# One eviction order for ScalarE in every slot of a hand-scheduled Flamingo-style block

## What is computed

```python
x = x + tanh(g0) * cross_attention_16_heads(layernorm(x), ctx)     # q, k, v projections, softmax, out projection
x = x + tanh(g1) * real(ifft(fft(layernorm(x)) @ w)) + bias        # becomes one 256x256 matrix, "fmix"
x = x + tanh(g2) * one_head_attention(layernorm(x), ctx, ctx)
t = rmsnorm(x); route = top 4 of 16 experts by t @ gate_w
x = x + tanh(g3) * sum over the 4 experts of route_e * mlp2_e(swiglu(mlp1_e(t)))
```

## Time and profile before

| | |
|---|---|
| median of 3 runs | 1135.19 us (1132.16 to 1136.17) |
| the profiled execution's own time | 1136.17 us |
| its span, first to last instruction | 1134.4 us, so 1.8 us lie around it |
| granted TensorE clock over the span | 0.98 |
| busy: TensorE, VectorE, ScalarE, GpSimd | 92%, 72%, 63%, 46% |

### The profile page before, as it was taken

One profiled execution on the slowest core, in us unless ns is written; L12 is line 12 of the kernel. 1 busy time (PEld: TensorE's weight loads), 2 busy tenths in 40 slices (PEclk: granted clock), 3 DMA queues, 4 the chain that ended last, 5 costly groups with the idle time before them and its releaser, 6 DMA issues. The chain is left out here.

```text
span 1134.4 us, 22413 instructions
## 1 busy us (share of the span) xinstructions
PE 1039.8 (92%) x7055; PEld 957.5 (84%) x7055; DVE 813.1 (72%) x2017; ACT 716.6 (63%) x1853; POOL 521.5 (46%) x747
## 2 busy tenths in 40 slices
PE   4899999999999999999999999999998778859995
PEld 4899898989889988889898988898897767858993
DVE  4656786868777787878686878677876865846665
ACT  4645766676766767676767676676766545635661
POOL 5413245445454635454545445463534225544441
PEclk9999999999999999999999999999998889989999
DMA  6332122222323232222222222212213522344469
GB/s 175 99 110 59 43 57 65 56 63 59 78 56 81 53 79 65 69 61 61 64 54 70 60 53 58 64 50 62 54 46 93 180 62 89 116 111 156 135 191 315
DMA packets 77569, 98.47 MB, mean 87 GB/s; under 512 B 14459, under 2 KB 69373, under 8 KB 77200
## 3 DMA queue, kind: packets, MB, share of 16 engines
q1 hardware_dynamic: 68064, 79.04, 26.3%
q0 software_dynamic: 8848, 16.96, 4.3%
q10 hardware_dynamic: 544, 1.05, 0.3%
HBM read 44.08 MB, written 23.03 MB: 59 GB/s over the span
## 5 line engine op out<-in xcount | busy, mean ns | idle before, releaser
L935 POOL TENSOR_TENSOR prob<-prob,rinv 112x750 f32<-112x750 f32 x128 | 184.1, 1438 | 250.3 <-DVE rinv L1609 239.8
L1027 ACT ACTIVATE prob<-ps_s,negmax 112x375 f32<-112x375 f32 x256 | 143.9, 570 | 61.5 <-DVE negmax L1603 52.4
L1616 DVE TENSOR_TENSOR pT_lo<-ps_pt,pT_hi 125x672 fp32r<-125x672 f32 x128 | 108.5, 847 | 63.1 <-ACT pT_hi L1164 57.7
L1707 PE MATMUL ps_kv<-ctxT_hi,wkv 128*128 128x376 f32 x512 | 138.5, 351 | 2.1 <-DVE v_lo L1276 1.4
L1603 DVE TENSOR_REDUCE negmax<-ps_s 112x2 f32<-112x750 f32 x128 | 119.0, 930 | 1.6 <-PE ps_s L1955 1.5
L1707 PE MATMUL ps_kv<-wkv,ctxT_hi 128*125 128x512 f32 x384 | 110.7, 410 | 2.4 <-DVE k_low L1272 2.4
L1017 ACT ACTIVATE v_hi<-ps_kv 125x512 fp32r<-125x512 f32 x96 | 57.3, 597 | 80.9 <-PE ps_kv L1707 75.8
L894 POOL DMA_INDIRECT places<-ysb,place_i x72 | 70.9, 984 | 81.1 <-issue 43.0
L1965 PE MATMUL ps_pt<-ident,prob 112*125 112x112 f32 x768 | 104.4, 272 | 2.3 <-POOL prob L935 2.3
L1164 ACT ACTIVATE pT_hi<-ps_pt 125x672 fp32r<-125x672 f32 x128 | 93.6, 731 | 5.7 <-PE ps_pt L1965 1.1
L1965 PEld LDWEIGHTS ps_pt<-ident,prob 112*125 112x125 f32 x768 | 94.8, 190 | 2.6 <-POOL prob L935 2.5
(11 more groups left out here) (312 smaller groups left out, 2752.8 us busy)
## 6 DMA issues: line engine op xcount, KB each, us to landing
kx<-k_low SPq DMA_DIRECT2D x256, 94.0 KB
xg<-rows_by_expert SPq DMA_DIRECT2D x72, 128.0 KB
qx_hi<-qx_hi SPq DMA_DIRECT2D x64, 112.0 KB, 2.2
zb<-places SPq DMA_DIRECT2D x16, 448.0 KB, 15.7
ctx_in<-in_ctx SPq DMA_DIRECT2D x16, 375.0 KB
stage_w<-in_L_ffn_mlp_w SPq DMA_DIRECT2D x16, 256.0 KB, 5.3
arena<-in_L_ffn_mlp_w SPq DMA_DIRECT2D x16, 256.0 KB, 5.8
stage_w<-in_L_xattn_w_kv SPq DMA_DIRECT2D x4, 512.0 KB, 11.9
```

What stands on the lines that cost most here:

```text
L935: e_prob.done(eng.tensor_tensor(prob[0:TQ, p % 2, :, :], prob[0:TQ, p % 2, :, :], rinv[:, 2 * p:2 * p + 2].unsqueeze(2).broadcast_to([TQ, ...
L1027: e_exp.done(eng.activation(prob[0:TQ, p % 2, half, :], S[0:TQ, half, 0:SK], ACT.Exp, bias=negmax[:, h:h + 1], accum_out=rowsum[:, h:h + 1]))
L1616: e_pt_lo.done(eng.tensor_tensor(pT_lo[:, :, :, :].rearrange("p h k t -> p h (k t)"), PT[0:KEYT, :, 0:NKEY * TQ], pT_hi[:, :, :, :].bitcas ...
L1707: last = eng.matmul(out_, lhs(i, k), rhs(j, k), start=(n == 1), stop=(n == KT * len(PASSES)))
```

## The change

ScalarE's program had two orders, by the parity of the slot. In even slots it did `oT`, `tail`, the expert tile, the projection evictions, then the exponents, then `pT_hi`. In odd slots it did `oT`, `tail`, exponents, `pT_hi`, the tile, the projection evictions. The change keeps the second order for all slots, and folds neighbouring loops over the pairs into one, on ScalarE, VectorE and TensorE:

```diff
@@ ScalarE @@
-                if g % 2 == 0:
-                    (oT of pair p)
-                    tail(g)
-                    for k in SLOT_TILES.get(g - LAST_BODY, ())[:1]:
-                        tile(k)
-                    for step, kind, n in kv_groups(g):
-                        projection(step, kind, n)
-                    (exponents of pair p)
-                    (pT_hi of pair p)
-                    tail_end(g)
-                else:
-                    (oT), tail(g), (exponents), (pT_hi), tile(k), projection(...), tail_end(g)
+                (oT of pair p)
+                tail(g)
+                for p in range(NP):
+                    st = due(g, AT_S[p])
+                    if st:
+                        exponents(st, p)
+                    st = due(g, AT_PT[p])
+                    if st:
+                        (pT_hi of pair p)
+                for k in SLOT_TILES.get(g - LAST_BODY, ())[:1]:
+                    tile(k)
+                for step, kind, n in kv_groups(g):
+                    projection(step, kind, n)
+                tail_end(g)
@@ VectorE @@
                         e_max.done(eng.tensor_reduce(negmax[:, 2 * p:2 * p + 2], S[0:TQ, :, 0:SK], AX.X,
                                                      ALU.max, negate=True))
-                for p in range(NP):
                     st = due(g, AT_S[p] + 1)
```

More of the change, by code:

```diff
@@ new lines, in _ @@
+                for p in range(NP):
+                    st = due(g, AT_O[p] + 1)
+                    if st:
+                        e_o.wait_ge(eng, st, p + 1)
+                        for half in range(2):
+                            rows_ = slice(64 * half, 64 * half + 64)
+                            last = eng.activation(oT[rows_, p, :], OT[rows_, half * TQ:(half + 1) * TQ],
+                                                  ACT.Copy)
+                        e_oT.done(last)
+                tail(g)
@@ new lines, in _ @@
+                for p in range(NP):
+                    st = due(g, AT_S[p])
+                    if st:
+                        exponents(st, p)
+                    st = due(g, AT_PT[p])
+                    if st:
+                        e_pt_pe.wait_ge(eng, st, p + 1)
+                        e_o.wait_ge(eng, st, p)
+                        e_pt_hi.done(eng.activation(
+                            pT_hi[:, :, :, :].rearrange("p h k t -> p h (k t)"),
+                            PT[0:KEYT, :, 0:NKEY * TQ], ACT.Copy))
```

## The result

The changed kernel takes 1161.08 us (median of 4, 1159.02 to 1163.83) against 1135.09 us (4 runs, 1132.16 to 1136.17): ratio 1.0239, 95% interval 1.0215 to 1.0262. It is slower, by 26 us where 7 were predicted. Its profiled execution took 1160.28 us with a span of 1158.5, so the two spans differ by 24.1 us.

What follows compares the result with a forecast made beforehand. TensorE was taken to bound the kernel; 15 rows x 0.4 = 6.0 us, first row 1.1 and slot 12 0 gave +7.1, or 1142 us against the median; forecast's own range 1139 to 1145, with rivals 1130 to 1149.

Steps and rivals of the forecast that it cites:

- Folded loops cost nothing, the exchange on ScalarE is all: All engines: folded loops keep their instruction order at no cost; only exponents going ahead of projection evictions in even slots remains.
- Slots 2 and 4, n1 late by 0.4 us: VectorE's delay from v2's late eviction reaches `x1` and n1: about 0.4 us a row, 6.0 us over 15 rows.
- the wait for `pT_lo` in slot 8: Sign of being right: a new TensorE wait in slot 8, where `pT_lo` had a margin of 0.05 us.
- First row +1.1 us: First batch row: GpSimd's L946 follows v2's late low part, so TensorE's wait for probabilities grows by 1.1 us.
- Slot 10: "nothing, with almost no margin": v5's eviction moves from 596.60 to about 597.9; its low part ends at about 599.2, bank wanted at 599.3.
- The `nT` wait stays, as slot 13's 0.57 us of idle time takes up the delay: ScalarE leaves slot 12 0.5 us late; idle time before q0's eviction absorbs it, leaving TensorE's slot 14 wait unchanged.
- a rival for gains: ScalarE's waits go away: `xnT` and `nT` waits of 11.1 and 6.7 us shrink, 1117 to 1130 us; chance 0.19.
- Slot 12: 0 to 0.1 us a row: c1's late eviction: low part ends at about 605.3, k0's product wants it at 605.33; summed as 0, bound 1.5 us.
- slots 10 and 12 hurt as well: Rival: c1's low part or v5's bank is late and the `nT` wait grows, another 7.5 us, 1150; chance 0.14.
- The rule that the prediction weighed for L1290: Slot 5's VectorE L1290 is held by GpSimd's L819 through shared SBUF ports: term stays 6 us, otherwise 1.5 us.

Runs made afterwards that it cites:

- x6: Kernel before, with the fourth choice's two scatters issued in slot 15, not 12, in all rows but the last; 1127.33 us, ratio 0.994.
- x1: Kernel before, with the new order (exponents ahead of evictions) in slot 10 alone; 1153.93 us, ratio 1.0152.
- x9: x7 with the new order in slot 10 alone; 1127.13 us, ratio to before 0.9941.
- x12: x7 with the new order in slots 6, 12 and 14 alone; 1136.2 us, ratio to before 1.0027.
- x8: Changed kernel with the scatters at x7's places; 1141.08 us, ratio to before 1.0089.
- x4: Changed kernel, with the row scatters of choices 2 and 3 issued in slots 14 and 15, entry scatters left in place; 1155.96 us, ratio 1.0168.
- x7: Kernel before, with second, third and fourth choice's scatters at offsets 43, 47, 48, not 42, 43, 44, except in the last row; 1121.01 us, ratio 0.9912.
- x13: x1 with the last choice's row scatter moved two slots later, to slot 14, its entry scatter left in slot 12; 1133.18 us, one run.
- x14: x13 plus a plain GpSimd write of the same 112 rows in the row scatter's old place; 1132.2 us, one run.

## Why the prediction was wrong, point by point

- *Folded loops cost nothing, the exchange on ScalarE is all*: right. The instruction sequences of all other engines are those of before.
- *Slots 2 and 4, n1 late by 0.4 us*: right. `x1` 0.36 late, TensorE +0.35 from slot 6 to 8 (0.4 predicted). TensorE gives all of it at n1, so the wait for `pT_lo` in slot 8, one of the prediction's signs, does not come.
- *First row +1.1 us*: too small. It went from 57.48 to 59.47 us. This row's interval 12 to 14 falls at about 8.5, 10.1 or 11.7 us (before 10.14, after 8.40, x6 11.74), whatever the order; without that interval the growth is 3.7 us.
- *Slot 10: "nothing, with almost no margin"*: **this is the step that failed.** Most of its numbers were right: v5's eviction 1.2 us late, `oT` unmoved. The bank of v5 had a little less than the margin that it needed. The context transposes that take it next start 6.15 us after the scores in place of 6.06, only 0.15 us behind the end of v5's low part. I put the +0.11 from 10 to 12 down to that, and in row 12 of after the profile names this wait (0.27 us for `v_lo`). But that is the small part. What I did not follow is VectorE behind v5's low part: its reciprocal for slot 11 is 1.22 us late, GpSimd's probabilities with it, and the two pairs of scatters that GpSimd issues behind them. I had asked of every moved instruction who wants its result, and not what is queued behind it on VectorE and then on GpSimd. The term stood at nothing and measured 0.94 us a row in the changed kernel. x1 gives the price alone, 17 us, and x9 shows that in a steady row it is paid only through those scatters.
- *The `nT` wait stays, as slot 13's 0.57 us of idle time takes up the delay*: wrong. That idle time, called a wait for q0's product, was the hold itself and grew to 1.32 us. The record of the `xnT` side had the same sign, and the prediction noted it ("what held it is not fully shown"), but built a rival for gains on it, not one for losses.
- *Slot 12: 0 to 0.1 us a row*: right for the bank (x12: 7.83 from 12 to 14 against 7.66, 0.17) and wrong beyond it: 0.45 us a row through `k_low` (x12), hidden in the changed kernel by the `nT` wait.
- *The rival "slots 10 and 12 hurt as well", 1150 at 0.14*, named the right place and the right wait. Its price of 0.5 us a row was half of the 0.94 measured, and its way, c1's low part or v5's bank, wasn't the one: v5's bank gave the 0.11.

The measured parts of a steady row, 0.35 + 0.11 + 0.94 = 1.40 us, would be 21 us over 15 rows. The body grew by 20.0. The first row gave more (1.99 us), rows 1, 2, 12 and 13 less (0.52, 0.73, 0.45 and 0.89); 2 and 12 of before (53.94 and 54.10 us) were held already. After the last score, after takes 258.6 us and before 254.0 (4.6 us; the first score comes 0.5 us sooner in after). There the granted clock was 0.90 in after and 0.95 in before. The windows from 900 us to the end, before and then after (stretch, us, busy of PE, PEld, DVE, ACT, POOL, clock, DMA share, GB/s):

```profile
900.00:1134.00 234.00, 190.37 (x1411) 175.29 (x1411) 148.34 (x383) 114.27 (x259) 96.44 (x105) 0.95 0.47 143
```

```profile
900.00:1158.00 258.00, 212.41 (x1514) 195.39 (x1512) 164.35 (x423) 125.91 (x286) 103.09 (x116) 0.90 0.47 148
```

The clock alone goes the right way, but the windows begin at different places of the program, and I ran nothing that isolates it. x8, with the changed order, has 254.9 us behind its last score and before 254.0, so the order itself doesn't need those 4.6 us. Over the runs, x4 left out, this stretch lies between 253.5 (x7) and 261.8 us (x12) without a pattern that I see. The cause of the 4.6 us stays open.

## What to carry to other kernels

When an instruction moves, follow its engine's queue past it until there is idle time, and then do the same on every engine that it feeds, up to the DMAs that they issue; the next user of the result is only one of the things that become late. An idle time that the profile puts down to a product already finished is not slack. Ask what else ends there, and see whether rows that differ in that other thing differ in the wait. Before giving up on a wait, try the transfers near it: other offsets in GpSimd's schedule gained 0.9%, when reordering ScalarE lost 2.4%.

## What the runs showed of the hardware

A hand-over from TensorE can be late while GpSimd has an indirect scatter under way. The q0 hand-over shows it in all 13 rows that have a routing beside them. ScalarE starts 2.02 to 2.16 us after the issue of the 112 KB row scatter in before and 1.90 to 1.96 us in after, and 1.73 to 1.84 us after that of the small entry scatter in x13 and x14. Without a scatter near it (the first rows of before), it starts 0.04 us after the product's end. A plain write of the same bytes from GpSimd does not do it (x14).

The late starts come from a late signal. The trace also records when an instruction's completion signal, its semaphore, is raised: for the two q0 products above at 606.38 and 620.28 us, 0.02 us ahead of ScalarE's starts. From 60 to 860 us of before there are 647 such signals of TensorE more than 2.5 us behind the last indirect scatter's issue, and none is over 0.02 us behind the modelled end of its matmul. Of the 181 nearer ones at least 45 are over 0.1 us late, up to 1.59 (32 can't be matched). So not every one is held. Here the k7 product ends at 595.16, 0.6 us behind an issue, and ScalarE takes it at once:

```profile
594.57 0.94 POOL L874 DMA_INDIRECT rows_by_expert<-row,at  x1 [0.31 <-issue]
594.65 0.51 PE L1707 MATMUL ps_kv<-ctxT_hi,wkv 128*128 128x376 f32 x2
...
595.20 0.48 ACT L1014 ACTIVATE kx<-ps_kv 128x376 fp32r<-128x376 f32 x1 [1.12 <-PE ps_kv L1707]
```

Hand-overs to VectorE can be hit too. In before this product ends at 703.16, and VectorE takes it 1.60 us later; two rows earlier it took the same product 0.31 us after its end (597.59 to 597.90):

```profile
702.62 0.93 POOL L874 DMA_INDIRECT rows_by_expert<-row,at  x1 [0.30 <-issue]
702.65 0.51 PE L1707 MATMUL ps_ot<-ctxT_hi,qk_lo 128*112 128x376 f32 x2
...
704.76 0.55 DVE L1416 TENSOR_REDUCE sm<-ps_ot 112x1 f32<-112x375 f32 x1 [0.86 <-remote]
```

L874's record lasts only 0.93 us. The Trainium skill, in "Perfetto Trace Analysis", section "DMA Instruction — SWDGE (GPSIMD)", states that this record ends when the descriptors are generated and not when the data has moved. No run here shows when the data of these scatters has moved; the trace shows only that the hold outlasts the record by 1 us. What in the chip holds the signal, and which condition picks the hand-overs that are hit, stays open.

A second thing: VectorE's L1382, a 112 x 1 operation, takes 0.16 us in before and 1.44 us in x7 and x12 (medians of 16), where it starts together with GpSimd's probabilities. In x7:

```profile
594.83 1.44 DVE L1382 TENSOR_TENSOR sm<-sm,gt 112x1 f32<-112x1 f32 x1
```

```profile
594.82 1.44 POOL L935 TENSOR_TENSOR prob<-prob,rinv 112x750 f32<-112x750 f32 x1 [1.31 <-DVE rinv L1609]
```

Both end within 0.01 us of 596.27. The rule that the prediction weighed for L1290 covers this one as well: by the Trainium skill, "SBUF — State Buffer", section "SBUF: two separate sides", a VectorE operation with two SBUF inputs waits for a GpSimd operation that reads SBUF and started first. The trace agrees (1.44 us against 0.16). That it takes away slack which would otherwise have absorbed part of slot 12's delay is my reading; no run tests it.
